# Where the row maxima are transposed in an attention step, and where their copy stands among the copies of the K stack

## The chip, the cores and the metric

The kernel runs on one core of one Trainium2 chip. The metric is the device time of the whole program in microseconds (us). A core has five engines that run their own instruction queues and meet only at semaphores: PE (matrix products and transposes), DVE (vector work), ACT (scalar engine), POOL (elementwise work) and SP (here it only issues DMA transfers).

## The reference

x and ctx are both 16 x 256 x 256 (batch, positions, channels), with 16 heads of 16 channels.

```
x = x + attention(layernorm(x), ctx, ctx)      # softmax(q k^T / 4) v, per head, no projections
x = x + ffn(layernorm(x))                      # w_down(silu(w_gate x) * (w_up x)), 704 hidden channels,
                                               # each operand rounded to FP4 in blocks of 16
```

The change touches only the attention part.

## The kernel before, in words

The program has two stages. The first, up to about 250 us of the span, is attention: one **step** per batch item, 16 in all, of about 14 us each. A step is written as 16 **slots** (g, j), g and j from 0 to 3, slot number 4g + j, one for each head. Each engine has its own `attention_step` that walks over the same 16 slots, so what stands in which slot is an order written out by hand for each engine. The second stage is the feed-forward network; nothing in it changes.

In slot h of step t, PE does the scores of head h of item t (L1095, `SC<-QS,KS`, two matmuls) and, right behind them, the scores whose maxima are wanted for a head 22 slots ahead (L1109, `MX<-KS,QS`, two matmuls). So slots 0 to 9 serve heads 6 to 15 of item t + 1, and slots 10 to 15 serve heads 0 to 5 of item t + 2. ACT takes the exponential of the scores (L630, `P<-SC`). DVE takes the maximum of each row (L802, `MF<-MX`). Two banks of `MX` are there: PE may write the bank of a slot once DVE has taken the maximum of two slots before. The scores have three banks `SC`. Four times in a step, in slots 3, 5, 10 and 15, PE multiplies the exponentials of four heads with the values (L1127, `PV<-P,VA`).

The maxima are subtracted inside the score product: two bf16 parts of the negated maxima are extra rows of the stacked operand `QS`. The way there, for item t + 1, in step t:

- DVE takes the last maximum in slot 9 and then writes the two parts (`maxima_high`, L823, and `maxima_low`, L828, both `MP`; the second signals `m_parts`).
- PE transposes the parts into the bank `TA` of `T` (`maxima`, L1064, two matmuls; waits for `m_parts` and for `o_norm`, since the same bank holds the transposed outputs of the item before until DVE has read them), in slot 11.
- ACT copies them to `MT` (`maxima_out`, L621), in slot 11.
- SP copies `MT` into rows 96 and 97 of `QS` by DMA (`QS<-MT`, L376, semaphore `m_stacked`).
- PE waits for `m_stacked` before the scores of head 0 in the next step.

Other work around it: `outputs` (L1074) transposes the attention outputs of the item before in slots 7 and 13; DVE normalises them (`denominators`, L836, `rden`; `output`, L842, `onrm`) in slots 9 and 13. `queries` (L1042 and L1049) splits the normalised queries of item t + 3 into three bf16 parts; ACT copies each out (L595, `QP<-T`). The keys of item t + 3 are split likewise into `KP`: parts 0 and 1 by ACT (L604 and L607, semaphore `k_out`), part 2 by POOL (L474, semaphore `k_low`). SP then spreads the parts over `KS` with six DMAs (`KS<-KP`) and, later in the step, over `QS` with six (`QS<-QP`), and loads the inputs of later items. All of SP's waits stand in one queue. In the profile several SP lines are given by the line of the `dma_start` or by L244, the helper `gate`.

The stacks of an item are needed by PE in slot 10 of the step after the one in which they are issued.

Of the kernel before, what the change touches and what calls it, by code (L numbers as in the profile page):

```python
# [35 lines left out]
IDENTS, CONSTS = 4, 9  # L36
AHEAD = 22
LEAD = 3
LOADS = 5
SCALE, GRID = 1, 0  # L40

# [51 lines left out]
def program(nc, x, x_p, ctx_in, ctx_t, wg_in, wu_in, wd_in, out):  # L93
# [8 lines left out]
    with es:  # L102
# [26 lines left out]
        KP = [sb(f"KP{r}", [128, 3, 512], bf16) for r in range(2)]  # L129
# [6 lines left out]
        KS, QS = [None] * RING, [None] * RING  # L136
# [70 lines left out]
        k_low, q_tr, m_tr, o_tr = sem("k_low"), sem("q_tr"), sem("m_tr"), sem("o_tr")  # L207
# [34 lines left out]
        def gate(eng):  # L242

            eng.sem_inc(passed, 1)  # L244
# [38 lines left out]
        @block.sync  # L283
        def _(sp):
            def load_first(b, r):
                sp.dma_start(QN[r][:, :, :, :, :].rearrange("p q e d a -> p q (e d a)"),
                             xp_d[:, bass.ds(b * QT, QT), :]).then_inc(qn_loaded[r], 16)
                sp.dma_start(KT[r][:, :], t_d[:, bass.ds(b, 1), :].rearrange("p a c -> p (a c)")).then_inc(kt_loaded[r], 16)

            def load_context(b, r):  # L290
                sp.dma_start(C[r][:, :, :], c_d[:, bass.ds(b * QT, QT), :]).then_inc(c_loaded[r], 16)

            def load_x(b, r):
                sp.dma_start(X1[:, tiles(b)].rearrange("p (q c) -> p q c", q=QT),
                             x_d[:, bass.ds(b * QT, QT), :]).then_inc(x_loaded[r], 16)

            def stack(dst, parts, order, r):


                for j, p in enumerate(order):  # L300
                    sp.dma_start(dst[j:PROD:6, :, :].rearrange("d h t -> d (h t)"),  # L301
                                 parts[:, p, :]).then_inc(stacked[r], 16)

            def load_blocks(m, w, lo, hi, done):
                sp.dma_start(WN[m][:, lo:hi, :], w[lo * 128:hi * 128, :].rearrange("(r p) c -> p r c", p=128)
                             ).then_inc(done, 16)

            def load_last(m, w, done):
                full = FI // 128
                sp.dma_start(WN[m][0:FI - full * 128, full, :], w[full * 128:FI, :]).then_inc(done, 16)  # L310

            def load_down(r, lo, hi, done):
                sp.dma_start(WD[:, r, lo:hi], wd_in[128 * r:128 * (r + 1), lo:hi]).then_inc(done, 16)

            PIECES = {t + 1: t for t in range(FI // 128 + 1)}
            DOWN = {7: (0, 0, 384), 8: (0, 384, FI), 10: (1, 0, 384), 11: (1, 384, FI)}

            def load_piece(t):

                done = w_piece[t % 3]  # L320
                if t in DOWN:
                    load_down(*DOWN[t], done)
                elif t in PIECES and PIECES[t] < FI // 128:
                    load_blocks(1, wu_in, PIECES[t], PIECES[t] + 1, done)
                elif t in PIECES:
                    load_last(1, wu_in, done)

            def piece_landed(t):

                turns = sum(1 for u in (*PIECES, *DOWN) if u <= t - 2 and u % 3 == (t - 2) % 3)  # L330
                if turns:
                    sp.wait_ge(w_piece[(t - 2) % 3], 16 * turns)
                sp.sem_inc(w_ready, 1)

            def part(dst, parts, p, rows, r):
                for j in rows:
                    sp.dma_start(dst[j:PROD:6, :, :].rearrange("d h t -> d (h t)"), parts[:, p, :]).then_inc(stacked[r], 16)

            def first_keys(b):

                for n, rows in enumerate(((0, 3, 5), (1, 4))):
                    sp.wait_ge(k_out, 2 * b + n + 1)
                    part(KS[b], KP[b], n, rows, b)
                sp.wait_ge(k_low, b + 1)
                part(KS[b], KP[b], 2, (2,), b)

            def first_queries(b):
                for n, rows in enumerate(((0, 1, 2), (3, 4), (5,))):
                    sp.wait_ge(q_out, 3 * b + n + 1)
                    part(QS[b], QP[b], n, rows, b)  # L350

            load_first(0, 0)
            load_first(1, 1)
            load_first(2, 2)
            first_keys(0)
            first_queries(0)
            first_keys(1)
            first_queries(1)
            load_context(0, 0)
            sp.wait_ge(w_zeroed, 4)  # L360
            load_blocks(0, wg_in, 0, 2, w_begun)
            load_first(3, 3)

            def attention_step(st):
                if st.has(LEAD):
                    r = st.slot(LEAD, RING)
                    sp.wait_ge(k_low, st.times(LEAD, 1, 1))
                    gate(sp)
                    sp.wait_ge(sc_ready, st.times(0, H, 1))
                    gate(sp)  # L370
                    stack(KS[r], KP[st.slot(LEAD, 2)], (0, 1, 2, 0, 1, 0), r)
                if st.has(1):
                    sp.wait_ge(mt_ready, st.times(1, 1, 1))
                    gate(sp)
                    r = st.slot(1, 2)
                    sp.dma_start(QS[st.slot(1, RING)][PROD:ROWS, :, :].rearrange("d h t -> d (h t)"),  # L376
                                 MT[r][:, :]).then_inc(m_stacked[r], 16)
                if st.first == -1:
                    load_context(1, 1)
                    load_blocks(0, wg_in, 2, 5, w_loaded)  # L380
                    load_last(0, wg_in, w_loaded)
                if 1 <= st.first + 1 < B:
                    piece_landed(st.first + 1)
                if st.has(LEAD):
                    sp.wait_ge(q_out, st.times(LEAD, 3, 3))
                    gate(sp)
                    stack(QS[r_q(st)], QP[st.slot(LEAD, 2)], (0, 0, 0, 1, 1, 2), r_q(st))
                if st.has(LEAD):
                    load_context(st.item(LEAD), st.slot(LEAD, RING))
                if st.has(LOADS):  # L390
                    load_first(st.item(LOADS), st.slot(LOADS, RING))
                if st.has(0):
                    load_x(st.item(0), st.slot(0, RING))
                load_piece(st.first)

            def r_q(st):
                return st.slot(LEAD, RING)

            def ffn_step(st):
                if st.has(-3):  # L400
                    r = st.slot(-3, 2)
                    sp.wait_ge(out_ready, st.times(-3, 1, 1))
                    gate(sp)
                    sp.dma_start(o_d[:, bass.ds(st.item(-3), 1), :].rearrange("p a c -> p (a c)"),
                                 OB[r][:, :]).then_inc(stored[r], 16)

            for t in range(-1, B + 1):
                attention_step(Step(t, B, RING))
            ffn_steps(sp, ffn_step)
            for r in range(2):  # L410
                sp.wait_ge(stored[r], 16 * (TILES // 2))
# [176 lines left out]
        def _(act):  # L588
# [68 lines left out]
            def attention_step(st):  # L657
# [5 lines left out]
                for g in range(NG):  # L663
                    for j in range(HG):
# [21 lines left out]
                        for n, at in enumerate(((2, 0), (2, 3), (3, 3))):  # L686
                            if (g, j) == at and st.has(LEAD):
                                part_out(QP[st.slot(LEAD, 2)], TB, n, q_tr, q_out, st)
                        if (g, j) == (2, 3) and st.first >= 0 and st.has(1):
                            maxima_out(st)  # L690
                        if (g, j) == (3, 1) and st.has(0):
                            evacuate(st, 0, 0)
# [98 lines left out]
        def _(dve):  # L791
# [89 lines left out]
            def attention_step(st):  # L881
# [3 lines left out]
                for g in range(NG):  # L885
                    for j in range(HG):
# [3 lines left out]
                            aggregate(st)  # L890
                        if (g, j) == ((1, 1) if st.first >= 0 else (3, 3)) and st.has(SCALE):
                            weight_maxima(st)
                        if (g, j) == (2, 1) and st.has(-1):
                            denominators(st, 0)
                            output(st, 0)
                        if (g, j) == (2, 1) and st.has(1):
# [139 lines left out]
        def _(pe):  # L1036
# [23 lines left out]
            def maxima(st):  # L1060
                pe.wait_ge(m_parts, st.times(1, 1, 1))
                pe.wait_ge(o_norm, st.times(-1, 2, 1))
                for q in range(QT):
                    last = nc.tensor.transpose(TA16[0:2 * H, q * 128:(q + 1) * 128],  # L1064
                                               MP[st.slot(1, 2)][:, q, :, :].rearrange("p a h -> p (a h)"), identb[:, :])
                last.then_inc(m_tr, 1)
# [83 lines left out]
            def attention_step(st):  # L1150
# [3 lines left out]
                for g in range(NG):  # L1154
                    for j in range(HG):
                        scores(st, g, j)
                        max_scores(st, g, j)
                        if (g, j) == (2, 2) and st.first < 0 and st.has(1):
                            maxima(st)
                        for n, at in enumerate(((2, 1), (2, 3), (3, 1)) if st.first >= 0 else ((2, 2), (3, 0), (3, 2))):  # L1160
                            if (g, j) == at and st.has(LEAD) and st.first > 1 - LEAD:
                                queries(st, n)
                        if (g, j) == (2, 3) and st.first == 1 - LEAD:
                            queries(st, 2)
                        if (g, j) == (2, 3) and st.first >= 0 and st.has(1):
                            maxima(st)
                        if (g, j) == (1, 3) and st.has(-1):
                            outputs(st, 0)
                        if (g, j) == (3, 1) and st.has(-1):
# [161 lines left out]
```

## Time and profile before

| | us |
|---|---|
| median of 3 runs | 531.93 |
| the three runs | 525.29, 531.93, 532.93 |
| the profiled execution, its time | 523.82 |
| the profiled execution, its span | 522.0 |

The span runs from the first to the last instruction, and all times in rows are counted from its start. The profile gives for each engine the busy time, for groups of instructions their count, busy time and idle time before them with what ended it, and for a stretch of time every instruction with its start and length. A row "start, us, engine, line, operation, out<-in, xcount" may merge several instructions of one kind; a bracket at its end is the idle time before it and what ended it. Matmuls are pipelined: a row of two matmuls of 256 columns has 0.38 us, but the next one starts 0.22 us later, so the distance from start to start is what PE needs.

### The profile page before, as it was taken

The page shows a single profiled execution, that of the slowest core. Times are in us where ns is not written, and L with a number is a line of the kernel's source. Part 1 is how long each engine was busy: PE and PEld are TensorE (multiplying, and loading weights), DVE is VectorE, ACT ScalarE, POOL GpSimd, SP SyncE. Part 2 cuts the span into 40 slices and gives each one's busy share as a digit, 9 for nine tenths or more (in the row PEclk, how much of TensorE's full clock was granted, in tenths as well). Part 3 has the DMA queues.
Part 4 walks back from the last instruction along what each step waited for, and adds up shares of the span by engine and source line. Part 5 has one row for each costly group of instructions (what it writes and reads, how often), then busy time and mean ns, then how long its engine had stood idle before and what let it go on. Part 6 is the DMA issues. An engine that isn't in the chain of part 4 may idle for free.

```text
span 522.0 us, 13665 instructions
## 1 busy us (share of the span) xinstructions
PE 486.6 (93%) x4036; PEld 383.8 (74%) x4036; DVE 431.3 (83%) x1081; ACT 373.7 (72%) x740; POOL 326.5 (63%) x471
## 2 busy tenths in 40 slices
PE   1889999999999999998858999999999999999996
PEld 0245666666665666655527899999999999999996
DVE  3778989999999999986456898889888998889764
ACT  5568989999999999977763556655665657655653
POOL 7846677667666667644444666666667666666442
PEclk9989999999999999999877999999999999999999
DMA  7764687777777667531000000000000000000000
GB/s 214 230 199 138 190 196 211 210 196 189 189 189 192 180 188 202 159 105 43 0 1 1 3 21 21 20 19 11 20 20 20 10 20 20 20 15 16 22 20 32
DMA packets 50321, 48.97 MB, mean 94 GB/s; under 512 B 4848, under 2 KB 48240, under 8 KB 50288
## 3 DMA queue, kind: packets, MB, share of 16 engines
q1 hardware_dynamic: 50288, 48.58, 33.0%
q8 instruction: 15, 0.25, 0.2%
q14 instruction: 18, 0.15, 0.1%
HBM read 18.94 MB, written 4.19 MB: 44 GB/s over the span
## 4 chain that ended last, share of the span: by engine, by line
PE 77%; DVE 7%; issue 5%; DMA 4%; ACT 3%; POOL 3%; SPq 1%; ACTq 0%; POOLq 0%; DVEq 0%
PE SC L1179 22%; PE PV L1179 12%; PE PV L1127 10%; PE MX L1109 10%; PE SC L1095 9%; DVE MF L802 4%; PE T L1204 4%; DMA QS<-MT 3%; PE T L1209 2%; PE T L1074 2%; PE T L1042 2%; PE SC L1204 1%; PE T L1049 1%; SPq L301 1%; PE SC L1209 1%
## 5 line engine op out<-in xcount | busy, mean ns | idle before, releaser
L802 DVE TENSOR_REDUCE MF<-MX 128x2 f32<-128x512 f32 x256 | 164.2, 683 | 20.8 <-PE MX L1109 17.1
L630 ACT ACTIVATE P<-SC 128x512 f32<-128x512 f32 x256 | 140.5, 594 | 20.2 <-PE SC L1095 18.3
L1109 PE MATMUL MX<-KS,QS 96*128 96x256 bf16 x512 | 103.7, 286 | 5.2 <-DVE MF L802 3.0
L1095 PE MATMUL SC<-QS,KS 98*128 98x256 bf16 x512 | 99.2, 276 | 2.0 <-DMA QS<-MT 1.8
L553 POOL TENSOR_TENSOR HQ<-HN,hscale 128x704 f32<-128x704 f32 x31 | 43.1, 1392 | 60.6 <-DVE HN L933 60.6
L735 ACT ACTIVATE HH<-T 128x768 fp32r<-128x768 f32 x31 | 25.2, 812 | 66.0 <-PE T L1204 66.0
L1127 PE MATMUL PV<-P,VA 128*32 128x256 f32 x1024 | 70.4, 393 | 0.9 <-ACT OT L639 0.9
L1095 PEld LDWEIGHTS SC<-QS,KS 98*128 98x128 bf16 x512 | 43.8, 98 | 34.6 <-ACT P L630 19.7
L1179 PE MATMUL SC<-WH,XH 128*128 128x352 f32 x256 | 68.5, 349 | 0.0
L1109 PEld LDWEIGHTS MX<-KS,QS 96*128 96x128 bf16 x512 | 45.1, 99 | 30.7 <-DVE MF L802 22.3
L1179 PE MATMUL SC<-WL,XH 128*128 128x352 f32 x256 | 62.9, 327 | 0.0
L1179 PE MATMUL SC<-WH,XL 128*128 128x352 f32 x256 | 62.9, 327 | 0.0
L1127 PEld LDWEIGHTS PV<-P,VA 128*32 128x32 f32 x1024 | 27.3, 111 | 25.9 <-ACT P L630 7.3
L1179 PEld LDWEIGHTS SC<-WL,XH 128*128 128x128 f32 x256 | 45.6, 192 | 0.0
L1179 PEld LDWEIGHTS SC<-WH,XL 128*128 128x128 f32 x256 | 45.3, 191 | 0.1
L540 POOL TENSOR_TENSOR HN<-HN,hinv 128x704 f32<-128x704 f32 x31 | 43.1, 1391 | 1.1 <-DVE hinv L1023 0.9
L1179 PEld LDWEIGHTS SC<-WH,XH 128*128 128x128 f32 x256 | 41.3, 194 | 1.6
L913 DVE TENSOR_TENSOR HN<-SC,SG 128x352 f32<-128x352 f32 x64 | 33.3, 520 | 10.7 <-PE SC L1179 9.5
L704 ACT ACTIVATE SG<-SC 128x352 f32<-128x352 f32 x64 | 29.4, 460 | 16.6 <-PE SC L1179 11.9
L548 POOL TENSOR_TENSOR frstd<-fve,mhalf 128x2 f32<-128x2 f32 x32 | 22.1, 691 | 29.3 <-DVE fve L980 29.3
L459 POOL TENSOR_TENSOR KR<-KT,KP 128x512 f32<-128x512 f32 x15 | 17.4, 1158 | 33.6 <-ACT KP L604 33.4
L595 ACT ACTIVATE QP<-T 128x512 bf16<-128x512 f32 x48 | 28.5, 595 | 6.6 <-PE T L1049 3.8
(138 smaller groups left out, 1039.5 us busy)
## 6 DMA issues: line engine op xcount, KB each, us to landing
KS<-KP SPq DMA_DIRECT2D x96, 128.0 KB, 3.3
QS<-QP SPq DMA_DIRECT2D x96, 128.0 KB, 2.4
QN<-in_x_p SPq DMA_DIRECT2D x16, 256.0 KB, 3.2
KT<-in_ctx_t SPq DMA_DIRECT2D x16, 256.0 KB, 4.5
C<-in_ctx SPq DMA_DIRECT2D x16, 256.0 KB, 3.1
X<-in_x SPq DMA_DIRECT2D x16, 256.0 KB, 4.8
out<-OB SPq DMA_DIRECT2D x32, 128.0 KB, 1.7
W<-in_L_ffn_w_up SPq DMA_DIRECT2D x5, 128.0 KB, 5.5
```

The source lines that it names most:

```text
L540: nc.gpsimd.tensor_tensor(blocks(HN[r][:, :]), blocks(HN[r][:, :]), each(hinv[r][:, :]), ALU.mult).then_inc(hm_ready, 1)
L553: nc.gpsimd.tensor_tensor(blocks(HQ[r][:, 0:FI]), blocks(HN[r][:, :]), each(hscale[r][:, :]), ALU.mult).then_inc(hq_ready, 1)
L595: nc.scalar.activation(parts[:, n, :], bank, ACT.Copy).then_inc(out_sem, 1)
L630: nc.scalar.activation(P[g % 2][:, j, :, :], SC[h % 3][:, :, :], ACT.Exp, scale=0.25).then_inc(exp_done, 1)
L704: nc.scalar.activation(SG[a][:, :], G, ACT.Silu).then_inc(silu_done, 1)
L802: nc.vector.tensor_reduce(MF[st.slot(off, 2)][:, :, h:h + 1], MX[h % 2][:, :, :], AX.X, ALU.max, negate=True).then_inc(mx_done, 1)
L913: nc.vector.tensor_tensor(HN[st.slot(0, 2)][:, a * FH:(a + 1) * FH], U, SG[a][:, :], ALU.mult).then_inc(h_done, 1)
L1095: last = nc.tensor.matmul(SC[h % 3][:, k, :], KS[r][0:ROWS, h, k * 128:(k + 1) * 128], QS[r][0:ROWS, h, :], start=True, stop=True)
L1109: last = nc.tensor.matmul(MX[h % 2][:, q, :], QS[r][0:PROD, h, q * 128:(q + 1) * 128], KS[r][0:PROD, h, :], start=True, stop=True)
L1127: last = nc.tensor.matmul(PV[32 * j:32 * (j + 1), g % 2, :], VA[r][:, k, HG * g + j, :], P[g % 2][:, j, k, :], start=(k == 0), stop=(k == ...
L1179: mm = nc.tensor.matmul(dst, x[:, c, :], w[:, c, :], start=(first and i == 0), stop=(last and i == len(chunks) - 1))
L1204: return nc.tensor.matmul(dst, src, ident[:, :], start=first, stop=False, is_transpose=True, skip_group_check=True)
```

## The change

Four edits, all in the attention stage:

1. DVE: `denominators` and `output` for the first half of the item before move from slot 9 to slot 8, that is from behind the last maximum to ahead of it. The parts of the maxima then stand right behind the last maximum.
2. PE: for steps 0 and later, `maxima` moves from slot 11 (behind `queries`) to slot 10, behind the products of that slot and ahead of `values`. In step -1 it stood there before.
3. ACT: for steps 0 and later, `maxima_out` moves from slot 11 to slot 10.
4. SP: the K stack is issued in two pieces. The copies of parts 0 and 1 (four of them) now wait for `k_out` in place of `k_low`; then comes the wait for `mt_ready` and the copy of `MT`; then the wait for `k_low` and the two copies of part 2.

```diff
+KEYS = (0, 1, 2, 0, 1, 0)
...
             def attention_step(st):
                 if st.has(LEAD):
                     r = st.slot(LEAD, RING)
-                    sp.wait_ge(k_low, st.times(LEAD, 1, 1))
+                    sp.wait_ge(k_out, st.times(LEAD, 2, 2))
                     gate(sp)
                     sp.wait_ge(sc_ready, st.times(0, H, 1))
                     gate(sp)
-                    stack(KS[r], KP[st.slot(LEAD, 2)], (0, 1, 2, 0, 1, 0), r)
+                    stack(KS[r], KP[st.slot(LEAD, 2)], KEYS, r, (0, 1, 3, 4))
                 if st.has(1):
                     sp.wait_ge(mt_ready, st.times(1, 1, 1))
...
+                if st.has(LEAD):
+                    sp.wait_ge(k_low, st.times(LEAD, 1, 1))
+                    gate(sp)
+                    stack(KS[r_q(st)], KP[st.slot(LEAD, 2)], KEYS, r_q(st), (2, 5))
...
-                        if (g, j) == (2, 3) and st.first >= 0 and st.has(1):
+                        if (g, j) == (2, 2) and st.first >= 0 and st.has(1):
                             maxima_out(st)
...
-                        if (g, j) == (2, 1) and st.has(-1):
+                        if (g, j) == (2, 0) and st.has(-1):
                             denominators(st, 0)
                             output(st, 0)
...
-                        if (g, j) == (2, 2) and st.first < 0 and st.has(1):
+                        if (g, j) == (2, 2) and st.has(1):
                             maxima(st)
...
-                        if (g, j) == (2, 3) and st.first >= 0 and st.has(1):
-                            maxima(st)
```

`stack` gets a last argument, the list of the rows of `KEYS` to copy.

How this moves the instructions, at the two places that matter. First PE, in a step of the loop, from the products of slot 10 to those of slot 12; before (six lines were added above, so line numbers differ by 6):

```order
L1109 MATMUL MX<-KS,QS 128x256 x2
L1127 MATMUL PV<-P,VA 32x256 x8
L1093 REGISTER_ALU
L1095 MATMUL SC<-QS,KS 128x256 x2
L1107 REGISTER_ALU
L1109 MATMUL MX<-KS,QS 128x256 x2
L1057 REGISTER_ALU
L1049 MATMUL T<-QP,negidentb 128x512
L1061 REGISTER_ALU
L1062 REGISTER_ALU
L1064 MATMUL T<-identb,MP 32x128 x2
```

and with the change:

```order
L1115 MATMUL MX<-KS,QS 128x256 x2
L1067 REGISTER_ALU
L1068 REGISTER_ALU
L1070 MATMUL T<-identb,MP 32x128 x2
L1133 MATMUL PV<-P,VA 32x256 x8
L1099 REGISTER_ALU
L1101 MATMUL SC<-QS,KS 128x256 x2
L1113 REGISTER_ALU
L1115 MATMUL MX<-KS,QS 128x256 x2
L1063 REGISTER_ALU
L1055 MATMUL T<-QP,negidentb 128x512
```

The transposes of the maxima's parts, with their two waits, passed one `PV` group, one pair of products and one query part: they now stand ahead of `PV`.

Second DVE, from the maximum of slot 8 to the parts; before:

```order
L802 TENSOR_REDUCE MF<-MX 128x2
L801 REGISTER_ALU
L802 TENSOR_REDUCE MF<-MX 128x2
L835 REGISTER_ALU
L836 RECIPROCAL rden<-T 128x16
L841 REGISTER_ALU
L842 TENSOR_TENSOR onrm<-T,rden 128x256
L823 CAST MP<-MF 128x2x16
L827 REGISTER_ALU
L828 TENSOR_TENSOR MP<-MF,MP 128x2x16
```

and with the change:

```order
L808 TENSOR_REDUCE MF<-MX 128x2
L841 REGISTER_ALU
L842 RECIPROCAL rden<-T 128x16
L847 REGISTER_ALU
L848 TENSOR_TENSOR onrm<-T,rden 128x256
L807 REGISTER_ALU
L808 TENSOR_REDUCE MF<-MX 128x2
L829 CAST MP<-MF 128x2x16
L833 REGISTER_ALU
L834 TENSOR_TENSOR MP<-MF,MP 128x2x16
```

The same six operations stand between the same neighbours; only the last maximum changed places with `rden` and `onrm`.

## Rows read from the trace of the kernel before

**Rows 1.** The page: busy time and share of each engine, matmul clock

```profile
PE 486.6 (93%) x4036; PEld 383.8 (74%) x4036; DVE 431.3 (83%) x1081; ACT 373.7 (72%) x740; POOL 326.5 (63%) x471
PEclk9989999999999999999877999999999999999999
```

**Rows 2.** One stretch: busy us of PE, PEld, DVE, ACT, POOL; clock, DMA

```profile
100.00:130.00 30.00, 29.63 (x313) 18.55 (x310) 27.74 (x62) 28.22 (x59) 21.48 (x35) 1.00 0.73 199
```

**Rows 3.** Who waited for the copy of the maxima: us, times (longest)

```profile
PEld SC L1095 <- DMA QS<-MT: 5.0, 8, 1.2
PE SC L1095: 1.8, 5
```

**Rows 4.** The chain that ended last: start, us, what

```profile
52.60 1.00 PE PV L1127 x16
...
73.89 3.34 DMA QS<-MT
...
89.42 2.29 DMA QS<-MT
...
96.14 1.00 PE PV L1127 x16
...
100.34 1.00 PE PV L1127 x16
...
110.15 1.00 PE PV L1127 x16
...
223.34 1.00 PE PV L1127 x16
```

**Rows 5.** Timeline, all engines, slots 10 to 12 of one step, and slot 0 of the next

```profile
97.72 2.61 DVE L802 TENSOR_REDUCE MF<-MX 128x2 f32<-128x512 f32 x4
...
99.96 0.38 PE L1109 MATMUL MX<-KS,QS 96*128 96x256 bf16 x2
...
100.27 1.07 PE L1127 MATMUL PV<-P,VA 128*32 128x256 f32 x16
...
101.37 0.19 DVE L828 TENSOR_TENSOR MP<-MF,MP 128x32 bf16<-128x32 f32 x1
...
101.73 0.38 PE L1049 MATMUL T<-QP,negidentb 128*128 128x512 bf16 x1
102.04 0.29 PE L1064 MATMUL T<-identb,MP 128*32 128x128 bf16 x2
102.25 0.39 PE L1095 MATMUL SC<-QS,KS 98*128 98x256 bf16 x2
...
102.67 0.36 ACT L621 ACTIVATE MT<-T 32x256 bf16<-32x256 bf16 x1
...
103.13 0.66 SPq L376 DMA_DIRECT2D QS<-MT  x1
...
105.77 0.39 PE L1095 MATMUL SC<-QS,KS 98*128 98x256 bf16 x2
...
106.42 2.49 DVE L802 TENSOR_REDUCE MF<-MX 128x2 f32<-128x512 f32 x4 [0.23 <-PE MX L1109]
```

**Rows 6.** Timeline: slot 10's product and the parts, an earlier step

```profile
56.43 0.38 PE L1109 MATMUL MX<-KS,QS 96*128 96x256 bf16 x2
...
57.54 0.19 DVE L828 TENSOR_TENSOR MP<-MF,MP 128x32 bf16<-128x32 f32 x1
```

**Rows 7.** Timeline: step -1, where PE waits for the parts

```profile
27.39 0.19 DVE L828 TENSOR_TENSOR MP<-MF,MP 128x32 bf16<-128x32 f32 x1
...
27.64 0.39 PE L1064 MATMUL T<-identb,MP 128*32 128x128 bf16 x2 [0.36 <-DVE MP L828]
```

**Rows 8.** SP's queue in the step that ends at 92 us

```profile
84.62 4.68 SPq L301 DMA_DIRECT2D KS<-KP  x6
```

**Rows 9.** PE's busy us and granted clock where it idles more

```profile
236.00:250.00 14.00, 11.26 (x113) 1.00 0.12 40
250.00:255.00 5.00, 4.96 (x42) 0.66 0.00 0
```

More of the change, by code:

```diff
@@ L295, in load_x, with stack @@
                              x_d[:, bass.ds(b * QT, QT), :]).then_inc(x_loaded[r], 16)
-            def stack(dst, parts, order, r):
-                for j, p in enumerate(order):
+            def stack(dst, parts, order, r, js=range(6)):
+                for j in js:
+                    p = order[j]
                     sp.dma_start(dst[j:PROD:6, :, :].rearrange("d h t -> d (h t)"),
```

## The prediction, as recorded before the changed kernel was run

> **What bounds the kernel now.** I read the page first: PE is busy 93% of the span, DVE 83%, ACT 72% [rows 1]. These are averages over two stages. The change lies in the attention stage, so I asked for stretches of that stage: in 30 us PE is busy 29.63, DVE 27.74 and ACT 28.22 [rows 2]. Three engines are nearly full, so a delay of one is soon a delay of all.
>
> Then the chain of waits. From 96 to 104 us it runs over PE alone, through products, value groups and transposes [rows 4]. PE sets the pace there, and whatever makes it stand still makes the step longer. The same view gives the length of a step as the distance between the value groups: 96.14 to 110.15 is 14.01 us, the shortest I found in full steps. From 52.60 to 223.34 twelve steps take 170.74 us, 14.23 each. So what disturbs the steps costs 12 x 0.22 = 2.6 us in all. The copy of the maxima is in this chain at many step boundaries, at 2.29 to 3.34 us from issue to landing [rows 4].
>
> Third, the waits for that copy: PE's weight loads 5.0 us in 8 times, its matmuls 1.8 us in 5 [rows 3], some of it at the same moments. So 6.8 us is the most that an earlier copy of `MT` can give back in this execution, and 2.6 us is what the lengths of the steps show of it.
>
> Last, the order of events around slots 9 to 11 in an undisturbed step [rows 5]. PE starts the product `MX` of slot 10 at 99.96 and is done issuing it 0.22 us later, at 100.18; the value group starts at 100.27. DVE takes four maxima without a gap from 97.72 on, then does `rden`, `onrm` and the two parts, and ends the last part at 101.37 + 0.19 = 101.56. PE's transposes of the parts start at 102.04, so in slot 11 the parts are there before PE is. **In slot 10 they are not**: PE comes to it at 100.18, 1.38 us before the parts exist. That is the distance on which the forecast rests.
>
> **The change, part by part.**
>
> *DVE's order.* The same operations stand between the maximum of slot 8 and the first part; one maximum and the pair `rden`, `onrm` only change places. DVE has no gap among them, so the second part still ends at 101.56. To have the parts earlier, `rden` and `onrm` would have to go behind them; they went ahead of the last maximum instead. I take nothing for it. The bounds: the first part now depends on the instruction just before it, which may add some 0.1 us (in step -1, where it also stands right behind the last maximum, nothing larger shows); and in some steps the parts already come sooner: there the distance is 57.54 + 0.19 - 56.43 - 0.22 = 1.08 us [rows 6]. Of the twelve steps 1 to 12, three have 1.08 or 1.09 and nine have 1.33 to 1.39. The rows shown are one of each kind.
>
> *PE: the transposes ahead of the value group.* From the end of the parts to the transposes passes 27.64 - 27.39 - 0.19 = 0.06 us where PE is waiting [rows 7]. The two transposes take 102.25 - 102.04 = 0.21 [rows 5], and the value group follows a product with a gap of 0.09 (100.27 against 100.18). So the value group starts at 101.56 + 0.06 + 0.21 + 0.09 = 101.92 in place of 100.27, 1.65 late. In slot 11 the transposes go away: 0.21 and the gap of 0.10 ahead of them (101.73 + 0.21 to 102.04), 0.31 together. From slot 12 on PE is 1.34 us late, which is the distance of 1.38 less 0.04.
>
> Who is behind the waiting instruction: the value group, then the products of slots 11 and 12. DVE has the product of slot 10 to work on, one maximum of about 0.65 us (2.61 / 4 [rows 5]), until 102.2. The product of slot 11 now comes after the value group: PE starts that slot at 101.92 + 1.01, and a maximum starts 106.42 - 105.77 = 0.65 after such a start, so at 103.6. DVE idles 1.4 us, and so does ACT, whose exponential of slot 11 needs the same group to pass. From slot 12 PE was the chain before and is it now, and in the next slot 0 DVE was already waiting for PE by 0.23 us [rows 5]. I see no gap on PE between slots 11 and 15 that could take up the delay. After slot 0 the pattern is that of before, shifted. So the step grows by the full amount.
>
> *Sum of this term.* Steps 1 to 12: 9 x 1.37 + 3 x 1.08 = 15.6. Steps 13 and 14 have fewer loads but the same order; I take them at 1.35 each, 2.7. Less 0.04 in 14 steps, 0.5. Step 0 has no output to normalise, and DVE ends the parts sooner; I give it 0.3. Together **+18.1 us**.
>
> *ACT.* `MT` is copied in slot 10. The transposes now end at about 102.2 and the copy can start 0.2 later where it started at 102.67 [rows 5]; it waits, but the next exponential could not start then anyway. A later exponential of slot 15 can hold the scores of slot 0 by up to 0.1 us a step, since they share a bank; 1.4 us in all is the upper bound and I take nothing.
>
> *SP: the K stack in two pieces.* With the copy of `MT` ready at 102.4 + 0.4, six K copies in one piece would end at about 103, just in front of it, as in the step where six took 4.68 us, until 89.30, and the copy of `MT` came 89.42 [rows 8, 4]. Four are out sooner, since they no longer wait for POOL's part. So `MT` goes out at about 102.8 in place of 103.13, or a little sooner. The two copies behind it and all six of the Q stack, then the loads, are queued behind the new wait for `mt_ready`; they are wanted in slot 10 of the next step, over ten slots later. Nothing for it.
>
> *What comes back.* The copy of `MT` lands at 102.8 + 3.34 at the latest, by the longest of [rows 4], 106.1. PE wants it at 105.77 + 1.34 = 107.1. The waits for it end: **-2.6 us**, with 0 and -6.8 as bounds. Most of this relief is because PE itself comes later.
>
> The rule in the Trainium skill, page "DMA: Bandwidth & Descriptors", section "Rules for kernel authors", is to issue a DMA early, compute, and wait for it late. By that rule alone the change would bring up to the 6.8 us of waits. The trace agrees that the waits exist; it is the price on PE that the rule leaves out.
>
> **Net: 18.1 - 2.6 = +15.5 us** on the profiled execution's own 523.82, so 539.3. That execution is 8.1 us faster than the median of the runs, 531.93. If those 8 us are more waiting for the same copy (then they vanish too), a slow run ends at 539 as well; if they lie elsewhere, at 547.4. I take **542**, nearer to the first.
>
> **Rivals.**
>
> *A. The wait on PE is paid in each step* (above). 79%. Its own range: 536 to 550.
>
> *B. Half of it is absorbed.* ACT and DVE have about 2 us of 30 free [rows 2], and the parts could come 0.3 us sooner in all steps, as in rows 6. Then +9 - 2.6, 530 on the profiled scale and up to 538 on the other: within 2%. Against it: the chain runs over PE, not over the engines that have the room. 9%.
>
> *C. Faster: the parts are not late.* DVE's new order would have to bring `m_parts` by 100.18, at which PE arrives; that is the point from which it decides, 1.38 us sooner than the rows show. Then only the gain stays, 2.6 to 6.8 us, or up to 15 if the slower runs wait for this copy: 517 to 529. 8%. Against it: DVE shows no gap it could close.
>
> *D. PE's new idle time lowers its clock.* PE has the full clock through the attention stage [rows 1, 2]; at the stage's end, after 11.26 busy in 14 us, a stretch of 5 us was granted 0.66 [rows 9], a mix of 1.2 and 2.4 GHz. At one such dip in each of 13 steps, each worth 0.34 x 5 = 1.7 us, the time would be 542 + 22 = 564. 4%. Against it: those 14 us themselves ran at 1.00 with 20% idle, and the new step has 1.4 in 15.4. The Trainium skill, page "TensorE: Matmul & The Clock Gate", section "HAM oscillation — how this bites in real kernels", describes kernels that fall back to the low clock at every wait; by it the time would be that of D if waits as short as these did so. No row here shows a dip after so short a wait.
>
> **How the numbers follow.** A measurement of this kernel tells about 2% from no change. The range of 80% is **531 to 552**: the low end takes the small distance in all steps and the whole 6.8 back (14 x 1.08 - 6.8 = +8.3, 532) and reaches into B; the high end is 547.4 with the 1.4 us of ACT and some scatter. Slower by over 2%: most of A, and D, 0.70. Within 2%: B and the low part of A, 0.23. Faster: 0.07.
>
> **What the profile of the changed kernel would show.** PE's wait for the parts (`T<-identb,MP`, released by DVE's `MP`) at some 14 places, over 1 us each; today the weight load shows it only where PE is idle anyway. A wait of DVE for `MX` of over 1 us behind the parts. Distances between value groups of about 15.4 us in place of 14.2. No waits for `QS<-MT`. The chain going through `MP` on DVE once in each step. The second stage unchanged. I am wrong if the parts end before PE has issued the product of slot 10, or if PE's wait is there and the steps still take under 14.5 us.

## The result, and the profile after

| | before | with the change |
|---|---|---|
| median of 4 runs, us | 528.61 | 540.95 |
| lowest to highest | 525.16 to 532.93 | 538.45 to 542.53 |
| the profiled execution, its time and span | 523.82, 522.0 | 540.41, 538.6 |

The ratio is 1.0225, with a 95% interval of 1.0118 to 1.0332: slower; whether by more than 2% these runs leave open. The kernel before was slower in these four runs than it mostly is: in three later groups of runs (25, 7 and 16) its medians were 525.74, 525.59 and 525.66, and 540.95 is 15.2 to 15.4 us above these. Later runs of the change without its SP edit gave 1.0268 (1.0215 to 1.0322). Forecast were 542 in a range of 531 to 552, and a difference of 15.5 us between the profiled executions; it is 16.6.

First the page of the changed kernel, which answers to [rows 1], and the stretch that answers to [rows 2]. The matmuls are the same 4036; PE is busy about as long, over a longer span.

```profile
PE 485.0 (90%) x4036; PEld 386.4 (72%) x4036; DVE 431.7 (80%) x1081; ACT 375.8 (70%) x740; POOL 327.0 (61%) x471
```

```profile
100.00:130.00 30.00, 27.11 (x287) 17.52 (x285) 25.87 (x56) 26.50 (x54) 19.70 (x33) 1.00 0.67 182
```

PE, DVE and ACT each lost 1.7 to 2.5 busy us of 30. No engine works longer on the same instructions; a step of 15.2 us holds the work of one of 14.0. That three engines all lose 6 to 9% of their busy time fits with waits of one for another. The waits (engine, line, who was waited for, us in total, times, longest) say where:

```profile
DVE MF L808 <- PE MX L1115: 30.4, 34, 4.6
...
PE T L1070 <- DVE MP L834: 19.1, 16, 1.9
PEld T L1070 <- DVE MP L834: 18.9, 13, 2.1
...
ACT MT L627 <- PE T L1070: 9.5, 15, 1.5
...
PEld SC L1101 <- DMA QS<-MT: 0.9, 1, 0.9
PE SC L1101 <- DMA QS<-MT: 0.4, 1, 0.4
```

PE waits 19.1 us for the second part of the maxima. DVE waits longer for PE's products than it did (30.4 us; before, 17.1). The waits for the copy of the maxima are down to 0.9 and 0.4 [rows 3]. The timeline of one step (start, us) shows the order of events that [rows 5] shows for before:

```profile
102.25 0.25 DVE L842 RECIPROCAL rden<-T 128x16 f32<-128x16 f32 x1
...
102.57 0.38 PE L1115 MATMUL MX<-KS,QS 96*128 96x256 bf16 x2
102.60 0.42 DVE L848 TENSOR_TENSOR onrm<-T,rden 128x256 f32<-128x256 f32 x1
102.94 0.68 DVE L808 TENSOR_REDUCE MF<-MX 128x2 f32<-128x512 f32 x1
...
103.97 0.19 DVE L834 TENSOR_TENSOR MP<-MF,MP 128x32 bf16<-128x32 f32 x1
...
104.22 0.23 PE L1070 MATMUL T<-identb,MP 128*32 128x128 bf16 x1 [1.27 <-DVE MP L834]
...
104.23 0.42 PE L1133 MATMUL PV<-P,VA 128*32 128x256 f32 x3
...
104.34 1.03 PE L1133 MATMUL PV<-P,VA 128*32 128x256 f32 x13
104.54 0.37 ACT L627 ACTIVATE MT<-T 32x256 bf16<-32x256 bf16 x1 [0.42 <-PE T L1070]
105.01 0.66 SPq L378 DMA_DIRECT2D QS<-MT  x1
...
105.30 0.39 PE L1101 MATMUL SC<-QS,KS 98*128 98x256 bf16 x2
...
105.95 1.35 DVE L808 TENSOR_REDUCE MF<-MX 128x2 f32<-128x512 f32 x2 [1.19 <-PE MX L1115]
105.97 0.38 PE L1101 MATMUL SC<-QS,KS 98*128 98x256 bf16 x2
```

PE has issued the product of slot 10 at 102.79; the parts end at 104.16, 1.37 us later, and PE stands still until 104.22. Then DVE, done with the one maximum it had, stands still for 1.19 us. In steps 1 to 13 the wait before the transposes is 1.23 to 1.36 us, in step 0 it is 0.23 and in step 14 1.85. The chain of waits of this step (start, us, what) runs through PE to 101.62, changes to DVE for the last maxima and the parts, and goes back to PE; before it stayed on PE [rows 4].

```profile
101.64 0.69 DVE MF L808
102.34 0.18 DVE rden L842
...
102.94 0.69 DVE MF L808
...
103.66 0.29 DVE MP L829
...
103.97 0.20 DVE MP L834
...
104.22 0.23 PE T L1070
104.45 0.92 PE PV L1133 x14
```

### The profile page after: what moved, and what is told of

It is laid out like the page before. It is cut to its first block, busy times and chain, and to the rows that moved or that the text cites. A ratio compares the mean times of both kernels' runs of the same rounds, so it can differ in the third digit from the quotient of the medians.

```text
span 538.6 us, 13679 instructions
## 1 busy us (share of the span) xinstructions
PE 485.0 (90%) x4036; PEld 386.4 (72%) x4036; DVE 431.7 (80%) x1081; ACT 375.8 (70%) x740; POOL 327.0 (61%) x471
## 4 chain that ended last, share of the span: by engine, by line
PE 76%; DVE 11%; issue 5%; ACT 3%; POOL 2%; SPq 2%; DMA 1%; DVEq 0%; POOLq 0%; ACTq 0%
PE SC L1183 22%; PE PV L1183 12%; PE PV L1133 10%; PE MX L1115 9%; PE SC L1101 8%; DVE MF L808 6%; PE T L1208 4%; PE T L1080 2%; PE T L1213 2%; PE SC L1208 1%; SPq L303 1%; PE T L1055 1%; PE T L1048 1%; DMA QS<-MT 1%; ACT P L636 1%
## 5 line engine op out<-in xcount | busy, mean ns | idle before, releaser
L808 DVE TENSOR_REDUCE MF<-MX 128x2 f32<-128x512 f32 x256 | 165.7, 683 | 33.2 <-PE MX L1115 30.4
L1101 PEld LDWEIGHTS SC<-QS,KS 98*128 98x128 bf16 x512 | 45.2, 98 | 32.5 <-ACT P L636 13.6
L1133 PEld LDWEIGHTS PV<-P,VA 128*32 128x32 f32 x1024 | 30.1, 111 | 20.6 <-ACT OT L645 5.1
L601 ACT ACTIVATE QP<-T 128x512 bf16<-128x512 f32 x48 | 29.6, 616 | 6.6 <-PE T L1055 3.8
```

The source lines that it names most:

```text
L601: nc.scalar.activation(parts[:, n, :], bank, ACT.Copy).then_inc(out_sem, 1)
L808: nc.vector.tensor_reduce(MF[st.slot(off, 2)][:, :, h:h + 1], MX[h % 2][:, :, :], AX.X, ALU.max, negate=True).then_inc(mx_done, 1)
L1101: last = nc.tensor.matmul(SC[h % 3][:, k, :], KS[r][0:ROWS, h, k * 128:(k + 1) * 128], QS[r][0:ROWS, h, :], start=True, stop=True)
L1133: last = nc.tensor.matmul(PV[32 * j:32 * (j + 1), g % 2, :], VA[r][:, k, HG * g + j, :], P[g % 2][:, j, k, :], start=(k == 0), stop=(k == ...
```

## The experiments

All against the kernel before on the same chip. The ratio is that of the kernel to the kernel before.

| kernel | median, us | ratio | 95% interval |
|---|---|---|---|
| SP edit alone | 521.31 | 0.9904 | 0.9866 to 0.9941 |
| change, parts of the step before | 524.36 | 0.9967 | 0.9938 to 0.9996 |
| change, transposes in front of slot 11's query part | 523.17 | 0.9938 | 0.9907 to 0.997 |
| change, transposes behind the value group | 526.92 | 1.0025 | 0.9997 to 1.0053 |
| change without the SP edit | 540.71 | 1.0268 | 1.0215 to 1.0322 |
| change without the DVE edit | 538.73 | 1.0262 | 1.0202 to 1.0321 |
| change in every other step | 532.35 | 1.0126 | 1.0079 to 1.0174 |
| SP edit alone, first piece late | 522.96 | 0.9937 | 0.9901 to 0.9972 |
| K stack all behind the copy of `MT` | 525.07 | 0.9983 | 0.9954 to 1.0011 |

The kernel before was at medians of 525.74, 525.59 and 525.66 in the three groups of runs. The rivals at the start: the early K copies, the place of the transposes as such, or the clock cost the time, and not the wait.

**1. The SP edit alone.** Against the change:

```diff
-                        if (g, j) == (2, 2) and st.first >= 0 and st.has(1):
+                        if (g, j) == (2, 3) and st.first >= 0 and st.has(1):
                             maxima_out(st)
...
-                        if (g, j) == (2, 0) and st.has(-1):
+                        if (g, j) == (2, 1) and st.has(-1):
                             denominators(st, 0)
...
-                        if (g, j) == (2, 2) and st.has(1):
+                        if (g, j) == (2, 2) and st.first < 0 and st.has(1):
                             maxima(st)
...
+                        if (g, j) == (2, 3) and st.first >= 0 and st.has(1):
+                            maxima(st)
```

> The SP edit alone (K stack in two pieces, the copy of MT between them); PE, ACT and DVE ordered as before. Theory (PE pays for the wait for the parts in slot 10): nothing of that wait is here, so the time is that of before within 2 us, 522 to 525 on the profiled scale (523.8); the copy of MT is less late in the three steps where the K stack held it up by 0.2 to 0.8 us. Rival (the early K copies collide with the loads of later items, and that made the change slow): this kernel carries most of the 16 us, 535 or more.

Measured: 521.31, faster than before by 1%, and 0.7 us below the 522 that was the low end expected: the edit gains more than was thought. Nothing of the loss is in this edit, and the rival falls. Its four runs lie within 520.9 to 521.95, and its steps are nearly all of the shortest length, 14.01 us: the chain holds the copy of `MT` once, where before it held it six times in the attention stage.

```profile
59.48 2.97 DMA QS<-MT
```

**2. The change without the wait.** PE transposes the other buffer, filled a step ago.

```diff
-                pe.wait_ge(m_parts, st.times(1, 1, 1))
+                pe.wait_ge(m_parts, st.times(1, 1, 1 if st.first < 0 else 0))
...
-                                               MP[st.slot(1, 2)][:, q, :, :]
+                                               MP[st.slot(1 if st.first < 0 else 0, 2)][:, q, :, :]
```

> The change, but PE transposes in slot 10 the parts of the step before (the other buffer of MP), so that it need not wait for the new ones; the maxima that are subtracted are therefore those of another item. All instructions and their places are those of the change. Theory: the wait for the parts goes; what is left in slot 10 is the wait for the normalised outputs, some 0.25 us a step; 14 times 1.1 us less than the change, 523 to 526. Rival (the place of the transposes ahead of the value group costs by itself, or the second stage's clock): 535 to 541.

Measured: 524.36 at the median of ten runs, 16.6 us less than the change. Same instructions, same places, only the dependence is gone; so the wait is the loss. What is left in slot 10 is a wait of some 0.23 us for the normalised outputs in most steps, and steps are 14.14 long (three of them from 189.25 to 231.66). The execution that was profiled took 529.22, because in one step of it PE waited long for a late copy of `MT`; that is told under the hardware, below.

**3. The transposes where the parts are just ready.** In slot 11, ahead of the query part; ACT copies `MT` ahead of `QP`.

```diff
-                        if (g, j) == (2, 2) and st.has(1):
+                        if (g, j) == (2, 2) and st.first < 0 and st.has(1):
+                            maxima(st)
+                        if (g, j) == (2, 3) and st.first >= 0 and st.has(1):
                             maxima(st)
```

> The change with PE's transposes in slot 11 ahead of the query part, and ACT's copy of MT in slot 11 ahead of the copy of the query part. Theory: PE comes there at 101.73 in the trace of before where the parts are ready at 101.62, so no wait; MT is copied 0.5 to 0.7 us sooner than before, and most waits for its DMA end: 2 to 3 us faster than before, 521 to 522. Rival (waits for the DMA were hidden anyway, or the later query part becomes the wait): 524 or slower.

Measured: 523.17 against 525.74, ratio 0.9938. The gain of 2.6 us is the one expected; the time is 1.2 us above the 521 to 522 expected, which had been counted from the profiled 523.82 and not from the median. It is no better than the SP edit alone. Steps are 14.02 long, as there, and of the 2.2 us between the two profiled executions 1.3 are there by the transposes of step -1 (29.00 for 27.72), ahead of anything that differs. Once the copy of `MT` is in time, having it earlier was worth nothing here.

**4. One place later than the change: behind the value group.**

```diff
-                        if (g, j) == (2, 2) and st.has(1):
+                        if (g, j) == (2, 2) and st.first < 0 and st.has(1):
                             maxima(st)
...
                             values(st, g)
+                        if (g, j) == (2, 2) and st.first >= 0 and st.has(1):
+                            maxima(st)
```

> The change with PE's transposes in slot 10 but behind the value group, one place later. Theory: PE comes there at 101.27 in the trace of before, 0.35 us before the parts can be used, so a fourth of the wait is left: 14 x 0.25 = 3.5 us more, less 2.6 us of DMA waits: 524 to 526. Rival (ACT's copy of MT in slot 10 holds the exponentials, wherever PE transposes): 532 or more.

Measured: 526.92, 14.0 us less than the change for one `PV` group's place, but 0.9 us above the 524 to 526 expected. The sum was short: twelve steps (58.11 to 230.44) are 14.36 us long on average, 0.3 more than with the SP edit alone, where 0.25 had been put in. ACT's copy of `MT` stands in slot 10 here as in the change, so ACT is not to blame. PE's matmuls wait for the parts 4.8 us in 15 times, or 0.3 each, where 0.35 was expected:

```profile
PE T L1070 <- DVE MP L834: 4.8, 15, 0.9
```

**5. The change without its SP edit.**

```diff
-                    sp.wait_ge(k_out, st.times(LEAD, 2, 2))
+                    sp.wait_ge(k_low, st.times(LEAD, 1, 1))
...
-                    stack(KS[r], KP[st.slot(LEAD, 2)], KEYS, r, (0, 1, 3, 4))
+                    stack(KS[r], KP[st.slot(LEAD, 2)], KEYS, r)
...
-                    stack(KS[r_q(st)], KP[st.slot(LEAD, 2)], KEYS, r_q(st), (2, 5))
```

> The change without its SP edit: the K stack goes out in one piece ahead of the copy of MT, once POOL's part is there. Theory: PE's wait in slot 10 sets the pace and the copy of MT has over a microsecond of room, so the time is that of the change within 2 us, 539 to 543. Rival (the SP edit hides the copy only because PE is late, and without it the copy is late again): up to 0.8 us more in some steps, 545 to 550.

Measured: 540.71, as expected. The SP edit, which gains 4.4 us by itself, gains nothing that these runs resolve where PE comes 1.2 us later anyway.

**6. The change without its DVE edit.**

```diff
-                        if (g, j) == (2, 0) and st.has(-1):
+                        if (g, j) == (2, 1) and st.has(-1):
                             denominators(st, 0)
```

> The change without its DVE edit: rden and onrm stand again between the last maximum and its parts. Theory: the same operations lie between the same neighbours, the parts end at the same moment, and the time is that of the change within 2 us, 539 to 543; perhaps 1 us less, since three steps before had the parts 0.3 us sooner. Rival (the new order brings the parts sooner and saves part of the wait): 545 or more.

Measured: 538.73 (537.72 to 541.96), 0.3 us below the range of 539 to 543 and inside it with the 1 us less that was allowed for; 2.2 us below the change's median. By the medians alone that could be scatter. The traces show a part of it: without the edit three steps have the parts 1.08 us after PE is ready, as before; with it all have 1.33 to 1.39. The edit, meant to bring the parts sooner, brings them 0.3 us later in three steps. Some 0.2 of it is the first part itself: right behind `onrm` it took 0.17 us in those three steps, right behind the last maximum 0.36. In the other nine it took about 0.4 before and 0.28 with the change. Why it was so short in just those three is not known.

**7. The change in every other step.**

```diff
-                        if (g, j) == (2, 2) and st.has(1):
+                        if (g, j) == (2, 2) and (st.first < 0 or st.first % 2 == 0) and st.has(1):
                             maxima(st)
...
+                        if (g, j) == (2, 3) and st.first >= 0 and st.first % 2 == 1 and st.has(1):
+                            maxima(st)
...
-                        if (g, j) == (2, 2) and st.first >= 0 and st.has(1):
+                        if (g, j) == (2, 2 + st.first % 2) and st.first >= 0 and st.has(1):
                             maxima_out(st)
```

> The change with the transposes and ACT's copy of MT in slot 10 in the even steps only, in slot 11 in the odd ones; DVE and SP as in the change. Theory (each step with the transposes in slot 10 pays 1.2 us by itself): half-way between the SP edit alone (521.3) and the change (541.0), 530 to 533, and the distances between the transposes alternate. Rival (the cost is one of a steady state, an engine that falls behind for good, or the clock): near one of the ends, 521 to 525 or 538 to 541.

Measured: 532.35; the middle of 521.3 and 541.0 is 531.1. Three transposes in a row in its timeline, in slots 10, 11 and 10:

```profile
73.51 0.23 PE L1070 MATMUL T<-identb,MP 128*32 128x128 bf16 x1 [1.26 <-DVE MP L834]
...
89.12 0.29 PE L1070 MATMUL T<-identb,MP 128*32 128x128 bf16 x2
...
102.72 0.23 PE L1070 MATMUL T<-identb,MP 128*32 128x128 bf16 x1 [1.28 <-DVE MP L834]
```

The pair of steps takes 29.21 us, 14.01 + 15.20. The wait is paid where it is made, once each, and nothing in the next step gives it back.

**8. Which half of the SP edit gains.** Against the SP edit alone:

```diff
-                    sp.wait_ge(k_out, st.times(LEAD, 2, 2))
+                    sp.wait_ge(k_low, st.times(LEAD, 1, 1))
```

> The SP edit alone (PE, ACT, DVE as before), but the first piece of the K stack waits for POOL's part as the whole stack did before; only the place of the last two K copies behind the copy of MT is new. What the SP edit gained is either the early start of four K copies, or the two copies fewer in front of the copy of MT. If the early start is what counts: the time of before, 524 to 526. If the order counts (SP is held up 1.3 us less, and two transfers fewer are under way when the copy of MT starts): 521 to 523, as with the SP edit alone.

Measured: 522.96, faster than before by 0.6%, and within the numbers given for the case that the order counts. SP now waits for `MT` in 15 of 16 turns, with the SP edit in all 16 and before in 7: the copy is seldom or never held up in the queue. That alone does not end the waits: in one step the copy took 4.02 us from issue to landing, and PE waited 1.4 us for it. Whether SP's shorter hold or the two transfers fewer under way is what gains, these runs do not part. That it is 1.6 us behind the SP edit alone is not resolved by these runs; the intervals overlap.

**9. The whole K stack behind the copy of `MT`.**

```diff
-                if st.has(LEAD):
-                    r = st.slot(LEAD, RING)
-                    sp.wait_ge(k_out, st.times(LEAD, 2, 2))
-                    gate(sp)
-                    sp.wait_ge(sc_ready, st.times(0, H, 1))
-                    gate(sp)
-                    stack(KS[r], KP[st.slot(LEAD, 2)], KEYS, r, (0, 1, 3, 4))
```

and all six copies behind `QS<-MT`, after waits for `k_low` and `sc_ready`. (The lines are those of the SP edit alone.)

> PE, ACT, DVE as before; the whole K stack is issued behind the copy of MT. If transfers under way in front of it are what makes the copy of MT late, this is the best order for it, and its waits go away altogether: 521 or a little less. If not, 523 to 526. The Q stack is issued 2.5 us later, which nobody waits for within ten slots.

Measured: 525.07, no different from before and 4 us above the 521 expected if nothing but the place of the `MT` copy counted. This expectation was wrong in its last sentence. The copy of `MT` is no longer in the chain, but the last Q copy is, three times, and PE's products of slot 10 wait for it:

```profile
PE MX L1110 <- DMA QS<-QP: 3.0, 3, 1.9
...
PEld MX L1110 <- DMA QS<-QP: 2.2, 1, 2.2
```

```profile
54.54 2.51 DMA QS<-QP
69.36 2.40 DMA QS<-QP
225.42 2.66 DMA QS<-QP
```

What is taken from in front of the copy of `MT` in SP's queue lands in front of the Q stack.

## Why the prediction was right, step by step

**The distance from PE's readiness to the parts.** Forecast 1.38 us in the undisturbed step, measured 1.37. Experiments 2, 4 and 7 show it as the cause: the dependence taken away, moved one place and halved in number, with the time following each.

**The delay per step.** Forecast 1.34, measured 1.2: twelve steps of the change, from the transposes at 58.18 to those at 241.03, take 182.85 us, and the same twelve with the SP edit alone 168.46. The term was 0.14 too large. From the product of slot 10 to the scores of slot 12 PE takes 3.40 us with the change (102.57 to 105.97) and 2.29 before (99.96 to 102.25, [rows 5]), so it is 1.11 late there and not 1.34. The missing 0.23 lies in one place: I had the scores of slot 11 start 1.31 us after the transposes (0.21 and a gap of 0.09, then a value group of 1.01), and they start 1.08 after them (104.22 to 105.30), since the first matmuls of the value group overlap the transposes (104.23). The rest of the 1.2 is lost later in the step, which the forecast had at nothing.

**DVE's new order at nothing.** Nearly: 0.3 us in three steps against it. The bound of 0.1 for a step was too small, and the three short distances that the sum counted at 1.08 had grown to 1.38. This and the item above partly cancel: the forecast for twelve waits, steps 1 to 12, was 15.1 us; measured over those of steps 2 to 13 are 14.4.

**What comes back.** Forecast 2.6 us, read from the lengths of the steps. The same twelve steps take 170.43 before and 168.46 with the SP edit alone: 2.0, by the trace. By the medians it is 4.4 (525.74 against 521.31), since the profiled execution was one of the better ones. The forecast left open whether the 8.1 us between it and the median were waits for this copy. Most of the 8.1 us were not there: the 531.93 was the median of three runs, and with 25 runs the median is 525.74, 1.9 above the profiled execution. Where the rest comes from stays open. One wait for the copy was left in the change (0.9 and 0.4 us, behind a copy that took 4.76 us to land), where the forecast had none. The four runs of the SP edit alone lie close together, but ten runs of experiment 2, with the same SP order, spread over 521.66 to 529.22.

**How good the 542 was.** PE's first product of the second stage starts at 275.00 before, at 272.19 with the SP edit alone and at 289.92 with the change. So by these three executions the waits on PE cost 17.7 us up to there for 18.1 forecast, the copies give back 2.8 for 2.6, and the net is 14.9 for 15.5. The sum holds. That the recorded 542 lies within 1.1 us of 540.95 is in part luck: it has 2.7 us in it for a slow median of the kernel before that later runs do not show, and the profiled execution of the change lost 1.7 us in the second stage, which comes next.

**SP's part.** Forecast as nothing beyond that; experiment 5 agrees for the change as a whole. That the edit gains when it stands alone was not asked in the forecast.

**The second stage unchanged.** The two profiled executions differ there, but not by the change. From PE's first product of that stage to the end of the span pass 247.0 us before (275.00 to 522.0) and 248.7 with the change (289.92 to 538.6). Over all eleven profiled executions of this document it is 246.8 to 247.6 us in six and 248.6 or 248.7 in five, and these do not sort by kernel: the change without its DVE edit, which has all the waits for the parts, takes 246.8, and experiment 9, which has them no more than the kernel before, 248.6. They sort by the granted clock in the first 25 us of the stage, 0.86 to 0.92 in the six and 0.83 or 0.84 in the five. These rows give the stretch, PE's, PEld's, DVE's, ACT's and POOL's busy time, and the granted clock, with the change and then without its DVE edit:

```profile
289.92:314.92 25.00, 21.21 (x117) 20.12 (x116) 17.84 (x55) 9.77 (x22) 12.44 (x19) 0.84 0.01 1
```

```profile
289.71:314.71 25.00, 21.21 (x129) 20.13 (x128) 18.81 (x58) 11.57 (x25) 13.90 (x20) 0.92 0.02 5
```

PE is busy as long in both and gets through 117 matmuls in one and 129 in the other. Why the clock falls further in one execution than in another is not shown.

**The rivals.** B (half absorbed) falls with experiment 7, C (parts not late) with the timeline. D (the clock falls at each wait) falls as a cause of the slowdown: in the profiled execution of the change the granted clock was 1.00 from 40 to 257 us, with a wait of 1.23 us or more in each step from 1 on. It does not fall altogether: in experiment 5, with the same waits, the clock went to 0.50 behind one of them, which is told below. Nor was the clock of before full through the whole stage, as the forecast had it: it was 0.66 from 35 to 40 us. Of the rule of the Trainium skill, page "DMA: Bandwidth & Descriptors", section "Rules for kernel authors", to issue a DMA early and wait for it late, experiment 1 is the good use: the copy of `MT` finds SP free, no engine is made to wait for the parts, and 525.74 becomes 521.31. The change applied it by moving an engine's work ahead of its input.

## What to carry to other kernels

Before an instruction is moved up in an in-order queue, read two times in the trace: when the engine would come to it in its new place, and when its input ends. If the input ends later, the difference is paid by all that stands behind it, in each turn; here three nearly full engines gave nothing back. The late transfer was better cured at its own queue, by what stands in front of it, as long as what is pushed back has room: moving two of six K copies gained 0.6%, or 1% with the other four started earlier as well, and moving all six gained nothing. And a profile is one execution: a difference of a microsecond or two behind the changed part may be the clock's, and is worth looking for in executions of other kernels before it is put down to the change.

## What the runs showed of the hardware that was not expected

A single wait can cost twice. In the profiled execution of experiment 2 one copy of `MT` landed 5.76 us after its issue, and PE waited. The PE timeline there (start, us):

```profile
75.06 1.07 PE L1133 MATMUL PV<-P,VA 128*32 128x256 f32 x16
78.62 0.47 PE L1101 MATMUL SC<-QS,KS 98*128 98x256 bf16 x2 [2.49 <-DMA QS<-MT]
78.88 0.64 PE L1115 MATMUL MX<-KS,QS 96*128 96x256 bf16 x2
79.31 0.63 PE L1101 MATMUL SC<-QS,KS 98*128 98x256 bf16 x2
...
82.01 1.94 PE L1133 MATMUL PV<-P,VA 128*32 128x256 f32 x16
...
85.13 0.63 PE L1115 MATMUL MX<-KS,QS 96*128 96x256 bf16 x2
85.69 1.07 PE L1133 MATMUL PV<-P,VA 128*32 128x256 f32 x16
86.69 0.39 PE L1101 MATMUL SC<-QS,KS 98*128 98x256 bf16 x2
```

And PE's busy time and granted clock in two stretches:

```profile
76.00:79.00 3.00, 0.51 (x7) 0.97 0.75 185
79.00:85.00 6.00, 6.00 (x37) 0.50 0.90 257
```

After the 2.49 us of idle the same products follow each other at 0.43 us in place of 0.22, and a value group takes 1.94 in place of 1.07: the granted clock was 0.50, which is 1.2 GHz and not 2.4, until about 85.7. This step took 19.54 us in place of 14.14 (70.66 to 90.20): 5.4 us for a wait of 2.5.

The length of the wait alone does not decide it. In the change, waits of 1.23 to 1.36 us in thirteen steps left the clock at 1.00. In the profiled execution of experiment 5 the same wait in the same place did so in twelve of them; behind the last the clock fell:

```profile
242.05 0.23 PE L1066 MATMUL T<-identb,MP 128*32 128x128 bf16 x1 [1.28 <-DVE MP L830]
```

```profile
240.00:242.00 2.00, 0.57 (x4) 0.13 (x2) 1.82 (x7) 0.90 (x2) 1.64 (x3) 1.00 0.06 17
242.00:246.00 4.00, 3.95 (x30) 2.46 (x31) 1.53 (x3) 1.57 (x3) 0.58 (x1) 0.57 0.21 70
```

From these transposes to the next it took 16.28 us (to 258.33), in the change 14.91 (241.03 to 255.94), 1.4 us more. In the change the clock fell, from 40 to 262 us, only behind the longer wait of step 14, 1.85 us, and was 0.50 from 258 to 260. So a wait on PE can cost more than its length, by 1.4 us and by 2.9 us in these two cases, and most waits of 1.3 us did not. What parts the one from the others is open, and so is whether such steps are behind the spread of the runs.
